# Raw weights loaded, rounded and split in two halves, at the end of a tile in routed layers 2 and 4, and three norms placed between the gathers

## What is computed

```python
nx = t5_layer_norm(h, ln2[i])
y = relu(nx @ ffn_wi[i]) @ ffn_wo[i]
if i in MOE_LAYERS:                       # layers 2 and 4 here
    top2, idx = top_k(nx @ gate_w, 2)
    y = y + sum over both of softmax(top2)[e] * (gelu(nx @ w1[e]) @ w2[e])
h = h + y
```

## Time and profile before

| | us |
|---|---|
| three timed runs | 1915.08, 1916.85, 1920.93 |
| their median | 1916.85 |
| the profiled execution | 1923.19 |
| its span, first to last instruction | 1921.40 |
| mean granted clock of PE over the span | 0.842 |

### The profile page before, as it was taken

One profiled execution on the slowest core, in us unless ns is written; L12 is line 12 of the kernel. 1 busy time (PEld: TensorE's weight loads), 2 busy tenths in 40 slices (PEclk: granted clock), 3 DMA queues, 4 the chain that ended last, 5 costly groups with the idle time before them and its releaser, 6 DMA issues.

```text
span 1921.4 us, 33734 instructions
## 1 busy us (share of the span) xinstructions
PE 1628.4 (85%) x11941; PEld 1507.5 (78%) x11941; DVE 1066.7 (56%) x2975; ACT 803.4 (42%) x1914; POOL 514.1 (27%) x1259
## 2 busy tenths in 40 slices
PE   5889996984988998999988999698989998899970
PEld 4878775984777997989877999588888997789970
DVE  3575555333645676557764443367755678434337
ACT  1444431433555554355433454245534544255420
POOL 2245334005422112612331000453235132300030
PEclk6766755995657999999889999779989989899985
DMA  4120101440097000100004666200010000256620
GB/s 143 32 78 10 42 20 49 149 159 26 23 284 223 1 2 27 53 1 6 15 28 141 205 217 199 71 15 1 1 63 18 1 15 16 63 180 214 210 88 26
DMA packets 78394, 149.76 MB, mean 78 GB/s; under 512 B 6340, under 2 KB 57843, under 8 KB 78230
## 3 DMA queue, kind: packets, MB, share of 16 engines
q1 hardware_dynamic: 71894, 135.35, 21.7%
q0 software_dynamic: 6336, 12.26, 2.2%
HBM read 106.59 MB, written 41.05 MB: 77 GB/s over the span
## 4 chain that ended last, share of the span: by engine, by line
PE 53%; issue 17%; DVE 16%; DMA 5%; ACT 5%; POOL 2%; SPq 1%; another core or an unknown queue 0%; DVEq 0%; POOLq 0%; ACTq 0%
PE ps_proj L1058 10%; PE ps_proj L1181 6%; PE ps_score L1252 6%; PE ps_proj L1072 5%; PE ps_o L1153 4%; PE ps_pt L1023 4%; PE ps_proj L1235 4%; PE ps_score L1109 4%; DMA w_in<-w_all_dram 4%; PE ps_o L1143 3%; PE ps_score L1120 2%; ACT w_hi L1400 2%; PE ps_proj L1039 1%; DVE prob L1581 1%; DVE negmax L1583 1%
## 5 line engine op out<-in xcount | busy, mean ns | idle before, releaser
L1252 PE MATMUL ps_score<-w,hid 128*112 128x192 f32 (+2 forms) x1680 | 305.5, 334 | 9.5 <-DVE x L1892 9.5
L1252 PEld LDWEIGHTS ps_score<-w,hid 128*112 128x112 f32 (+2 forms) x1680 | 277.8, 180 | 11.8 <-DVE x L1892 11.1
L1376 ACT ACTIVATE hid<-ps_proj 128x224 f32<-128x224 f32 (+2 forms) x360 | 133.8, 382 | 266.8 <-PE ps_proj L1235 253.9
L1481 POOL TENSOR_SCALAR tmp<-rs,var 111x1 f32<-111x1 f32 x110 | 40.9, 372 | 626.8 <-DVE rs L1552 626.3
L1439 POOL DMA_INDIRECT tin<-rows_out,idx x66 | 68.3, 1035 | 482.9 <-issue 377.1
L1023 PE MATMUL ps_pt<-const,prob 111*111 111x111 f32 x660 | 128.3, 313 | 36.7 <-ACT probt L1364 24.9
L1181 PE MATMUL ps_proj<-wo,ot 128*111 128x192 f32 (+1 forms) x616 | 143.5, 384 | 3.9 <-ACT ot L1342 3.7
L1023 PEld LDWEIGHTS ps_pt<-const,prob 111*111 111x111 f32 x660 | 96.2, 205 | 57.1 <-issue 25.9
L1364 ACT ACTIVATE probt<-ps_pt 111x333 f32<-111x333 f32 x176 | 78.9, 448 | 130.2 <-PE ps_pt L1023 128.8
L1181 PEld LDWEIGHTS ps_proj<-wo,ot 128*111 128x111 f32 (+1 forms) x616 | 115.6, 209 | 15.6 <-issue 12.8
L1153 PEld LDWEIGHTS ps_o<-v,probt 111*111 111x111 f32 x1056 | 127.3, 193 | 0.4
(11 more groups left out here) (255 smaller groups left out, 4212.9 us busy)
## 6 DMA issues: line engine op xcount, KB each, us to landing
w_in<-w_all_dram SPq DMA_DIRECT2D x65, 768.0 KB, 4.2
w<-w_all_dram SPq DMA_DIRECT2D x50, 576.0 KB, 5.1
rows_in<-zero SPq DMA_DIRECT2D x1, 12320.0 KB, 47.0
rows_out<-zero SPq DMA_DIRECT2D x1, 9240.0 KB, 79.2
tin<-rows_in SPq DMA_DIRECT2D x36, 224.0 KB
rows_out<-tout SPq DMA_DIRECT2D x36, 168.0 KB
patch<-patches_dram SPq DMA_DIRECT2D x11, 333.0 KB, 3.0
wo<-wo_all_dram SPq DMA_DIRECT2D x6, 576.0 KB, 3.9
```

What stands on the lines that cost most here:

```text
L1252: last = pe.matmul(bank[0:n, 0:C], hid[:, i % 2, m, at:at + n], w2[:, slot, m, :], start=(m == 0), stop=(m == FC - 1))
L1376: act.activation(hid[:, i % 2, m, 0:n], bank[:, 0:n], ACT.Relu if b.tile is None else ACT.Gelu).then_inc(taken, 1)
```

## The change

- **Halves.** A load of raw weights becomes two DMAs of 768 columns each, with a semaphore each. ACT rounds each half when it has landed, in two instructions; DVE splits each behind its rounding. SP issues half 0 of the next load when half 0 is split (`w1_half`) and half 1 when half 1 is split (`w1_ready`). This holds for every load of the kernel. The expert's number is now read once ahead of both waits.
- **Place.** In layers 2 and 4, tile 0 keeps a `W1` behind chunk 2, and in each tile `W1 r + k + 3` stands behind chunk 5, ahead of part 1 of the down-projection (in the first of the last dense blocks behind it). So a tile's weights are rounded one tile and a bit ahead. SP's part is a step of its own, `LD`, right behind each `W1`.
- **End of layer 2.** Three gathers stand ahead of the last dense block instead of four. `COMB` 0 to 2 follow from chunk 4 on with no `GAT` between, the last down-projections come ahead of `next A`, and `GAT` 3 to 6 stand behind `next A` 1 and 2. Layer 4 keeps its order of gathers.

```diff
--- before.py
+++ after.py
@@ -439,25 +439,29 @@
             out.append(("U", 2 + k, m))
             if m == 2 and k + 1 < n:
                 out.append(("X", k + 1))
-            if m == 2 and (k < n or not last):
-                out.append(("W1", r + k + 2))
+            if m == 2 and k == 0:
+                out.append(("W1", r + 2))
+            ahead = [("W1", r + k + 3)] if m == 5 and k + 3 <= n + (1 if last else 3) else []
+            if k < n:
+                out += ahead
             if k and m in (2, 5):
                 out.append(("D", 1 + k, m // 3))
-    out += [("GAT", 0), ("GAT", 1), ("GAT", 2), ("GAT", 3)]
+            if k == n:
+                out += ahead
+    out += [("GAT", 0), ("GAT", 1), ("GAT", 2)] + ([("GAT", 3)] if last else [])
     for m in range(FC):
         out.append(("U", 3 + n, m))
         if m % 2:
             out.append(("D", 2 + n, m // 2))
-        if m >= (1 if last else 2) and (last or m < 5):
-            g = m - (1 if last else 2)
-            out += [("COMB", g), ("GAT", g + 4)]
-        if m == 2 and not last:
-            out.append(("W1", r + n + 3))
-    out += [] if last else [("W1", r + n + 4), ("next", ("A", 0))]
+        if last and m:
+            out += [("COMB", m - 1), ("GAT", m + 3)]
+        if not last and m > 3:
+            out.append(("COMB", m - 4))
     out.append(("D", 3 + n, 0))
-    out += [] if last else [("next", ("A", 1))]
+    out += [] if last else [("COMB", 2)]
     out.append(("D", 3 + n, 1))
-    out += [] if last else [("next", ("A", 2))]
+    out += [] if last else [("next", ("A", 0)), ("next", ("A", 1)), ("W1", r + n + 4), ("GAT", 3), ("next", ("A", 2)),
+                            ("GAT", 4), ("GAT", 5), ("GAT", 6)]
     if last:
         for g in range(5, G):
             out.append(("COMB", g))
@@ -492,7 +496,8 @@
         steps = att_order(st[1], every[i - 1], follower) if st[0] == "att" else ffn_order(st[1], follower is None)
         for x in steps:
             out.append((follower, x[1]) if x[0] == "next" else (every[i - 1], x[1]) if x[0] == "prev" else (st, x))
-    return out
+
+    return [x for st, step in out for x in [(st, step)] + ([(st, ("LD", step[1] + 1))] if step[0] == "W1" else [])]
 
 
 PROGRAM = program()
@@ -713,8 +718,9 @@
         late_in = sem("late_in")
         patch_in = [sem(f"patch_in{i}") for i in range(PATCH_RING)]
         wo_in = sem("wo_in")
-        w1_raw = sem("w1_raw")
-        w1_rounded = sem("w1_rounded")
+        w1_raw = [sem(f"w1_raw{i}") for i in range(2)]
+        w1_rounded = [sem(f"w1_rounded{i}") for i in range(2)]
+        w1_half = sem("w1_half")
         w1_ready = sem("w1_ready")
         w2_in = [sem(f"w2_in{i}") for i in range(FW_RING)]
         spare_ready = sem("spare_ready")
@@ -824,8 +830,6 @@
                 if second and n >= FW_RING:
 
                     sp.wait_ge(score_full, LAST_D[DOWN[n - FW_RING]] + 1)
-                elif r >= 1 and not second:
-                    sp.wait_ge(w1_ready, r)
                 w = w2_all if second else w1_all
                 if source == "run":
                     src = w[at]
@@ -836,7 +840,10 @@
                     sp.dma_start(w2[:, n % FW_RING, :, :].rearrange("p m c -> p (m c)"),
                                  src).then_inc(w2_in[n % FW_RING], 16)
                 else:
-                    sp.dma_start(w1_in[:].rearrange("p c n -> p (c n)"), src).then_inc(w1_raw, 16)
+                    for c, split in enumerate((w1_half, w1_ready)):
+                        if r:
+                            sp.wait_ge(split, r)
+                        sp.dma_start(w1_in[:, c, :], src[:, c * F:(c + 1) * F]).then_inc(w1_raw[c], 16)
 
             def next_load(r):
                 if r < NLOADS and LOADS[r][1:] != ("tile", 0):
@@ -926,9 +933,9 @@
                     sp.wait_ge(stats_ready, NORMS[(("att", NEIGH), "XA", G - 1)] + 1)
                     load_w(DOWN[0], True)
                     load_w(DOWN[1], True)
-                elif kind == "W1":
-                    next_load(step[1] + 1)
-                    if step[1] == LOAD0[("att", T5)] + 1:
+                elif kind == "LD":
+                    next_load(step[1])
+                    if step[1] == LOAD0[("att", T5)] + 2:
                         later_fill()
                 elif kind == "TAB":
                     sp.wait_ge(table_ready, TABLE_F.index(st[1]) + 1)
@@ -1026,7 +1033,7 @@
             def att_step(st, step):
                 a = st[1]
                 s = ATTS[a]
-                if step[0] in ("NX", "BD", "QS", "XA", "LATE", "W1", "ND"):
+                if step[0] in ("NX", "BD", "QS", "XA", "LATE", "W1", "LD", "ND"):
                     return
                 kind, g = step[0], step[1]
                 key = (st, *step)
@@ -1393,11 +1400,13 @@
                     turned_rows(st, step[1])
                 elif kind == "W1":
                     r = step[1]
-                    act.wait_ge(w1_raw, 16 * (r + 1))
+                    act.wait_ge(w1_raw[0], 16 * (r + 1))
                     if r >= W_RING:
 
                         act.wait_ge(proj_full, LAST_PROJ[r - W_RING] + 1)
-                    act.activation(w1_hi[:, r % W_RING, :, :], w1_in[:], ACT.Copy).then_inc(w1_rounded, 1)
+                    act.activation(w1_hi[:, r % W_RING, 0, :], w1_in[:, 0, :], ACT.Copy).then_inc(w1_rounded[0], 1)
+                    act.wait_ge(w1_raw[1], 16 * (r + 1))
+                    act.activation(w1_hi[:, r % W_RING, 1, :], w1_in[:, 1, :], ACT.Copy).then_inc(w1_rounded[1], 1)
 
         @block.gpsimd
         def _(pool):
@@ -1737,10 +1746,11 @@
                 elif kind == "W1":
 
                     r = step[1]
-                    dve.wait_ge(w1_rounded, r + 1)
+                    dve.wait_ge(w1_rounded[0], r + 1)
                     slot_w = r % W_RING
-                    link(dve.tensor_tensor(w1_lo[:, slot_w, 0, :], w1_in[:, 0, :],
-                                           w1_hi[:, slot_w, 0, :].bitcast(F32), ALU.subtract))
+                    tell(dve.tensor_tensor(w1_lo[:, slot_w, 0, :], w1_in[:, 0, :],
+                                           w1_hi[:, slot_w, 0, :].bitcast(F32), ALU.subtract), w1_half, r + 1)
+                    dve.wait_ge(w1_rounded[1], r + 1)
                     tell(dve.tensor_tensor(w1_lo[0:64, slot_w, 1, :], w1_in[0:64, 1, :],
                                            w1_hi[0:64, slot_w, 1, :].bitcast(F32), ALU.subtract), w1_ready, r + 1)
                 elif kind == "S":
```

## The result

Five runs of the changed kernel gave a median of 1890.76 us (1880.07 to 1893.67), beside 1915.08 for the kernel before (1899.40 to 1920.93, five runs): ratio 0.9872, 95% interval 0.9841 to 0.9904, so 24.3 us less by the medians. The forecast was 1899 with a range of 1891 to 1908. The sign and the places were right; the time lies 0.2 us under the low end, and on the gain the forecast was some 6 us short.

A forecast was written before the change was run, and what follows sets the result against it. The prediction took the closed circle of w_in loads to bound the tile loops and POOL's queue the end of layer 2. Loops -16.6, first tiles +6.0, smaller costs +0.9 and +0.3, norms -8.4 gave -17.8: 1899 us, range 1891 to 1908.

The forecast's parts named there:

- The circle: Tile loop: issue, landing, rounding, splits and next issue of w_in cannot overlap; 8.42 us against PE's own 7.93.
- The rounding's cover: Tile loop: ACT's rounding of the halves (1.66 us) hides under part 1 of the down-projection with 0.5 us of cover.
- rival 1: Tile loop keeps its period: down weights landing 6.3 us after issue, or late rounding; chance, half or more lost, 0.13.
- A half's landing: Tile loop: a 384 KB half of w_in lands 3.2 us after its issue, near the 3.0 of 333 KB patches.
- rival 2: Tile loop slower: halves land in series, half 1 after 7.4 us, circle 9.6 us; total 1953 us; chance 0.04.
- The loops: Tile loops of layers 2 and 4: PE becomes the bound, 16 periods each 0.51 and 0.53 us shorter, -16.6 us.
- The first tiles: Layers 2 and 4: early rounding holds ACT, PE waits at chunk 2 of tile 1; +3.0 us each, +6.0 together.
- The end of layer 2: POOL, first gather to group 2's norm: three gathers instead of six, 18.8 us for 27.23, so -8.4 us.
- rival 4: End of layer 2: the gathers are only put off and the 8.4 us paid in the attention; 1907.4 us; chance 0.06.
- The sum: Whole kernel: -16.6 + 6.0 + 0.9 + 0.3 - 8.4 = -17.8 us, giving 1899 us.
- SP's extra DMA and the other loads: One more SP issue ahead of the first tokens, +0.9 us; longer rounding in layer 0 and attention stages, +0.3 us.
- how the numbers follow: Closing step: 0.3% (5.8 us) can be told from no change; faster means under 1911, chance 0.91; range 1891 to 1908.

The follow-up runs named there:

- halves alone: Kernel before plus halves and the number read ahead, with layers 2 and 4 and the end of layer 2 in the old order: 1896.07 us, ratio 0.9893.

## Why the prediction came out as it did

**The circle** was read rightly: issue, landing, rounding, splits, reading, issue. With it PE became the bound at 7.92 us, where 7.93 was forecast. What was not seen is which link carries the edit. The number read ahead of the wait went into the sum as 0.1 instead of 0.74 us of SP's answer, a detail of the halves; it is enough alone for most of the loop's gain (111.5 us of 14 tiles, against 119.5 before and 110.9 with halves).

**The rounding's cover** under part 1 was put at 0.5 us and is 0.68; the end of the splits, 3.5 us after the start of part 1, is at 3.33; the down weights go 5.78 us after it, as forecast (5.8). They land in layer 2's loop after 5.4 us, 5.9 at most, below rival 1's 6.3, and nothing waits for them. The row of SP's loads of w_in and of w there, time to landing:

```profile
DMA to landing us min/median/max: 2.9/3.7/6.2
...
DMA to landing us min/median/max: 4.4/5.4/5.9
```

**A half's landing** was put at 3.2 us, near the 333 KB of the earlier trace rows. It is 3.5 on the page and 3.7 in the loop. Taken apart, half 0 lands in layer 2's loop after 3.0 to 3.6 us (median 3.1), as forecast, and half 1, issued 1 us later with half 0 still under way, after 3.7 to 4.7 (median 4.1); one pair issued 0.5 us apart took 5.6 and 6.2. Half 1 was mis-sized by 0.9 us, and it is the one whose circle counts: 1722.39 - 1720.08 + 4.1 = 6.4 us, 1.5 below the period, so it cost nothing, and rival 2 is out. On the page weighed there: the Trainium skill, "DMA: Bandwidth & Descriptors", section "Anatomy of one DMA", gives 2.9 us by its fit for 384 KB, an estimate; the page gives the fit for DMAs issued by GpSimd, and these are issued by SP, so here the measured 3.5 decides.

Its advice in section Bandwidth to batch to 1 MiB or more, on a table for the same path, can be set beside a stretch of 90 us: the kernel before, halves alone, the changed kernel.

```profile
1060.00:1150.00 90.00, 85.31 (x621) 82.67 (x620) 36.58 (x63) 44.87 (x96) 0.00 (x0) 1.00 0.65 213
```

```profile
1060.00:1150.00 90.00, 90.00 (x663) 88.28 (x662) 39.21 (x67) 49.43 (x113) 0.00 (x0) 1.00 0.72 225
```

```profile
1060.00:1150.00 90.00, 90.00 (x661) 88.38 (x660) 40.12 (x69) 49.51 (x114) 0.00 (x0) 1.00 0.76 229
```

For each byte the DMA engines are busy 5% longer with halves alone and 9% longer in the changed kernel. By the same stretch of the other profiles it is 2 to 6% in the four with halves in the old place and 8 to 9% in the three of the changed kernel, so by the means about half of it goes with the halves and the rest with the new place. PE was busy all the time in both.

**The loops** were put at 16 periods of 0.51 and 0.53 us, -16.6. Measured: -7.9 and -9.4 for 14 tiles, -1.2 on layer 2's way to the gathers and -0.6 on layer 4's, -19.1. The term was some 2.5 us too small and the measured value lies outside its own bounds (0 to -17.5), since a single profile of before had the shorter of the two lengths that layer 4's loop takes there (118.9 and 121.7); against that profile alone it is -17.1.

**The first tiles** were put at +3.0 each and measured at +3.6 and +4.0, within the range of +3 to +8 for both. The wait is the one forecast, at chunk 2 of tile 1 (3.27 us, named as 2 to 3). The clock is the part that varies: 0.54 over the 10 us that hold the wait in the second profile of the changed kernel, 0.83 in the first, and the 2 tiles take 20.7 or 19.3 us. In the first it was 0.51 for the 3 us behind the wait, in the second it had fallen before the wait ended and was 0.50 for 6 us more. I took 0.4 us for it of 0 to 1.4. The rows of the first profile, then of the second:

```profile
1030.00:1040.00 10.00, 6.73 (x39) 6.43 (x39) 3.17 (x5) 4.04 (x9) 0.00 (x0) 0.83 0.49 171
```

```profile
1040.00:1050.00 10.00, 7.27 (x32) 6.89 (x32) 3.17 (x5) 3.55 (x8) 0.00 (x0) 0.54 0.46 154
```

**The end of layer 2** was put at -8.4 (range -5 to -9): the norms measured -8.6, QK stands 2.28 us behind instead of 2.06, and the gathers put off are covered, so rival 4 is out. The 2.2 us given back behind norm 2 were not in the sum. They are 0.5 us in the first profile of the changed kernel and 3.0 in the other two, which have the gap of PE shown above (1.3 us). Behind that gap the granted clock falls to 0.50. The rows show it, the first profile without the gap and then the second, at the same distance from norm 2:

```profile
1213.00:1215.00 2.00, 2.00 (x15) 1.94 (x14) 0.00 (x0) 1.25 (x3) 0.00 (x0) 1.00 0.00 0
```

```profile
1224.00:1226.00 2.00, 2.00 (x9) 2.00 (x8) 0.00 (x0) 0.45 (x1) 0.00 (x0) 0.50 0.00 0
```

The 12 matmuls from 1223.22 to 1226.67 follow each other at 0.28 us instead of 0.16, some 1.5 us more by my estimate; with the gap that is 2.8 of the 3.0. What opens the gap the trace does not name.

**The sum** of the stretches, -17.3, thus stands close to the forecast's -17.8, the errors of the terms (-2 for the loops, +1.6 for the first tiles, +2.2 behind the norms, and 1.2 us forecast for SP's extra DMA and the other loads, which lie outside the table) nearly cancelling: that the sum fits is in part luck. The measured -24.3, -19.4 and -23.5 us by the medians are 2 to 7 more. What makes up that rest is not settled. By the mean ratio it is 4.5 us; each ratio's interval is some 6 to 7 us to either side, so that of a mean of three some 4. Without the stretches of the table, the slow start's 8 us and DVE's wait near the end, the profiles' spans are 1550 and 1550 us before and 1539, 1555 and 1546 changed: 3 us less by the means, beside 16 between profiles of one kernel.

**The step that failed** is the loops' term and, behind it, the last step, how the numbers follow. The circle that the term stands for is as forecast; its size is not: -16.6 with -17.5 as its bound, where the runs showed -19.1. These 2.5 us are more than the 0.2 us by which the time lies under the range. The range was built from the terms' bounds and the rivals: all terms at their low ends give 1893 (0.9 + 3.0 + 0.9 + 0.3 + 0.6 below 1899), and for the 2 us from there to 1891 the prediction names no reason. It had no term for the measurement: single executions of the kernel before lay between 1899 and 1930 us, and its median moved between 1910.7 and 1923.7 from chip to chip, while the forecast took the median of three runs as fixed and "about 0.3%" as what can be told. With 1915.08 in place of 1916.85 the same sum gives 1897; the low end of 1891 left 6 us for everything else. About 6 us to either side for the measurement, added as squares to the range's own -8 and +9, would have given 1889 to 1910.

## What to carry to other kernels

When a buffer is alone in a loop, add up the circle of its own issue, landing, use and release, and compare it with the busiest engine's period; then shorten its cheapest link first, which here was a register read that could stand ahead of a wait. Halving the buffer's work buys room against late transfers. Moving the work to a place with "more cover" can cost at the loop's start and, with the circle still closed, loses outright (1.0083 here). And a range for a total needs a term for the spread of the measurement, taken from single executions, beside the terms of the edit.

## What the runs showed of the hardware

- Reading a register from memory and computing the address on SP before a DMA whose place depends on it cost 0.56 us of SP's answer (0.74 to 0.18 us) when it stood behind the wait.
- In two otherwise equal starts the granted clock was 0.50 and 0.84 over 15 to 40 us, and the first output came 8 us later in the slow one.
- One DVE instruction near the end waited 6.5 to 9.4 us in eight of thirteen profiles and not at all in five, alike within each of the three groups of runs, but not in the first pair of profiles; what ends it the trace does not name.
- In two profiles of the changed kernel PE stopped for 1.3 us at a granted clock of 1.00 in the first attention work behind layer 2; the clock fell to 0.50 some 1.4 us after it had gone on, for about 3.4 us. In the first profile, where it did not stop, the clock stayed at 1.00.
- Of two transfers of 384 KB issued 1 us apart, the first landed after 3.0 to 3.6 us and the second after 3.7 to 4.7 (5.6 and 6.2 in one pair issued 0.5 us apart), where single ones of 768 KB took 4.1 to 4.6 in the kernel before.
- The DMA engines were busy 2 to 6% longer for each byte with loads of 384 KB in place of 768 KB (share 0.72 for 225 GB/s, 0.65 for 213).
